# Query stores that wait for stack loads and maximum rows, batch 0's queries loaded in halves, and a subtraction behind two maxima, in a four-layer gated cross-attention network

## The reference

```python
x = x + jnp.tanh(g_xattn[0]) * _L0_xattn_ref(_layernorm(x), ctx, ctx, mask)
x = x + jnp.tanh(g_ffn[0])   * _L0_ffn_ref(_layernorm(x), ...)
x = x + jnp.tanh(g_xattn[1]) * _L1_xattn_ref(_layernorm(x), ctx, ctx, Wq, bq, Wk, bk, Wv, bv, Wo, bo)
x = x + jnp.tanh(g_ffn[1])   * _L1_ffn_ref(_layernorm(x), ...)     # 8 experts, 2 per token
...                                                                # layers 2 and 3 likewise
# the attention core of every layer:
scores = jnp.einsum('bqhd,bkhd->bhqk', q, k) * scale               # layer 0 also masks
attn = jax.nn.softmax(scores, axis=-1)
x = jnp.einsum('bhqk,bkhd->bhqd', attn, v)
```

## Time and profile before

| | |
|---|---|
| time, median of 3 runs | 1563.36 us (1557.87, 1563.36, 1565.05) |
| the profiled execution | 1561.88 us, its span 1560.0 us |
| PE busy | 1321.7 us, 85% of the span |
| PE weight load busy | 958.7 us, 61% |
| DVE busy | 963.4 us, 62% |
| ACT busy | 861.6 us, 55% |
| POOL busy | 714.5 us, 46% |
| chain that ended last | PE 68%, DVE 13%, DMA 6%, ACT 6%, issue 4% |
| mean granted TensorE clock | 0.933 of full speed |

### The profile page before, as it was taken

The page is one execution under the profiler, slowest core; times in us unless marked ns, Lnnn a source line. Parts: engine busy times, 40 slices in busy tenths (PEclk is TensorE's granted clock), DMA queues, the critical chain, the costliest instruction groups (busy, mean ns, idle before and its releaser), DMA issues.

```text
span 1560.0 us, 29423 instructions
## 1 busy us (share of the span) xinstructions
PE 1321.7 (85%) x9524; PEld 958.7 (61%) x9524; DVE 963.4 (62%) x2651; ACT 861.6 (55%) x1718; POOL 714.5 (46%) x843
## 2 busy tenths in 40 slices
PE   2599989987999489999999799848999388995985
PEld 1355479954666279999986466627887245664433
DVE  6589753335895743333337598575554277967787
ACT  2266764424887145555545488535555155885564
POOL 4366440003742677776741474258994415622000
PEclk9999999997999699999999799959999796997998
DMA  9989130048761333334147975124444498710001
GB/s 268 285 146 159 23 99 1 1 129 200 132 136 60 108 122 122 117 112 162 69 156 230 216 140 108 35 85 143 153 134 170 152 275 165 141 33 1 0 14 41
DMA packets 115568, 188.86 MB, mean 121 GB/s; under 512 B 21296, under 2 KB 91568, under 8 KB 109232
## 3 DMA queue, kind: packets, MB, share of 16 engines
q0 software_dynamic: 37056, 105.19, 28.7%
q1 hardware_dynamic: 78368, 81.79, 17.0%
HBM read 128.17 MB, written 50.20 MB: 114 GB/s over the span
## 4 chain that ended last, share of the span: by engine, by line
PE 68%; DVE 13%; DMA 6%; ACT 6%; issue 4%; POOL 1%; SPq 1%; ACTq 0%; DVEq 0%; POOLq 0%
PE PS L1212 10%; PE PS L1232 10%; PE PS L1053 9%; PE PS L1008 8%; PE PS L1012 3%; PE PS L1224 3%; DMA qk_parts<-q_parts 3%; PE PS L1090 2%; PE PS L1033 2%; PE PS L1026 2%; PE PS L1066 2%; DMA stack<-qk_parts 1%; PE PS L894 1%; PE PS L880 1%; DVE act L2593 1%
## 5 line engine op out<-in xcount | busy, mean ns | idle before, releaser
L2108 DVE TENSOR_REDUCE nm<-PS 128x2 f32<-128x512 f32 x384 | 249.9, 676 | 37.0 <-PE PS L1008 35.7
L1008 PE MATMUL PS<-stack 48*128 48x256 f32 x1024 | 214.2, 335 | 52.6 <-DVE q_parts L2043 16.2
L1008 PEld LDWEIGHTS PS<-stack 48*128 48x128 f32 x1024 | 152.9, 206 | 136.1 <-issue 57.8
L1012 PE MATMUL PS<-stack 49*128 49x256 f32 x1024 | 203.7, 321 | 0.9 <-ACT probs L1533 0.6
L1232 PE MATMUL PS<-weights,hh 128*128 x936 | 189.5, 292 | 4.5 <-DVE hl L2435 4.3
L1212 PE MATMUL PS<-weights,xh 128*128 x468 | 171.2, 421 | 11.8 <-DVE xl L2419 5.2
L680 POOL DMA_DIRECT2D stack<-mt x128 | 73.3, 573 | 216.0 <-ACT mt L1542 212.0
L1533 ACT ACTIVATE probs<-PS 128x512 f32<-128x512 f32 x256 | 145.1, 595 | 41.2 <-PE PS L1033 23.8
L1533 ACT ACTIVATE xng<-PS 128x512 f32<-128x512 f32 x256 | 145.3, 595 | 22.0 <-PE PS L1033 16.0
L1232 PEld LDWEIGHTS PS<-weights,hh 128*128 128x128 f32 x936 | 152.6, 193 | 6.5 <-issue 6.0
L1012 PEld LDWEIGHTS PS<-stack 49*128 49x128 f32 x1024 | 143.0, 195 | 10.4 <-ACT probs L1533 4.6
(11 more groups left out here) (329 smaller groups left out, 3079.3 us busy)
## 6 DMA issues: line engine op xcount, KB each, us to landing
stack<-qk_parts POOLq DMA_DIRECT2D x128, 256.0 KB, 4.1
qk_parts<-stack SPq DMA_DIRECT2D x32, 512.0 KB, 7.0
qk_parts<-q_parts SPq DMA_DIRECT2D x32, 512.0 KB, 8.3
stack<-qk_parts POOLq DMA_DIRECT2D x128, 128.0 KB, 3.8
weights<-W_dram POOLq DMA_DIRECT2D x12, 1024.0 KB
wide<-ctxT_dram SPq DMA_DIRECT2D x16, 512.0 KB, 9.4
wslot<-y_tokens SPq DMA_DIRECT2D x16, 512.0 KB, 7.5
weights<-W_dram POOLq DMA_DIRECT2D x12, 512.0 KB
```

Source lines behind the costliest of these rows:

```text
L1008: mm = pe.matmul(PS[:, u % 3, to], nat_q[:, at], nat_k, start=True, stop=True)
L1012: mm = pe.matmul(PS[:, 3 + v % 3, to], key_k[:, at], key_q, start=(l > 0 or half == 0), stop=(l > 0), skip_group_check=(l == 0))
L2108: nc.vector.tensor_reduce(nm[:, j % 2, at:at + 2], PS[:, (2 * t + h) % 3, :].rearrange("p (q n) -> p q n", q=2), AX.X, ALU.max, negate=Tru ...
```

## The change

1. **Stores held.** In layers 1 to 3 `store_q` of q1 waits for a new semaphore `stack_first` (the batch-0 keys, the ones and the first half of batch 0's queries have landed). The first part of q2 waits for maximum row 0, the second for row 1; those of q3 for rows 2 and 3. SP also waits for the store of group g - 2.
2. **Where q1's parts lie.** In layers 1 to 3 they lie in `probs` (`q_part`). So q3's high part no longer waits for q1's store (`q_place`); the first exponential does now.
3. **Halves.** In all layers batch 0's query portions are loaded by `load_queries` in two halves of four pairs of heads: 8 DMAs of 64 and 128 KB in place of 4 of 128 and 256 KB. PE's unit 0 waits for the first half, unit 8 for the second.
4. **Low part moved.** In layers 1 to 3 DVE's low part of q3 stands behind the first two maxima, and PE waits for it at the first transpose of maxima, not at unit 0.

```diff
@@ store_q (SP)
                 sp.wait_ge(qhi_done, GROUPS * l + g + 1)
                 sp.wait_ge(qlo_done, GROUPS * l + g + 1)
-                for r, part in enumerate((q_hi(g), q_lo(g))):
+                if l and g >= 2:
+                    sp.wait_ge(*stored(q_out, l, g - 2))
+                for r, part in enumerate((q_hi(l, g), q_lo(l, g))):
+                    if l and g == 1 and r == 0:
+                        sp.wait_ge(stack_first, 144 * (l + 1))
+                    if l and g >= 2:
+                        j = QUADS * l + 2 * (g - 2) + r
+                        sp.wait_ge(row_in[j % 4], 16 * (j // 4 + 1))
                     sp.dma_start(rows_of(0, r, g), by_batch(part)).then_inc(q_out[g % 2], 16)
@@ q_part, q_place (new)
+        def q_part(l, g, r):
+            if l and g == 1:
+                return probs[:].rearrange("p a n -> p (a n)").rearrange("p (r c n) -> p r c n", r=2, c=KC)[:, r].bitcast(F32R)
+            return q_parts[:, g % 2, r]
+        def q_place(l, g):
+            return stored(q_out, l, g - 4 if l and g == 3 else g - 2)
@@ load_queries (POOL, new; stands for load_stack(l, 0, 2) and load_stack(l, 0, 3))
+            def load_queries(l):
+                pool.wait_ge(*stored(q_out, l, 0))
+                for half in range(2):
+                    cs, landing = slice(PAIRS // 2 * half, PAIRS // 2 * (half + 1)), stack_in[0] if half else stack_first
+                    for h in range(2):
+                        rows = lambda r, n: stack[64 * h + DH * r:64 * h + DH * (r + n), 0, 0, cs].rearrange("p c n -> p (c n)")
+                        part = parts[0, 0, h, 0, :, cs].rearrange("p c n -> p (c n)")
+                        nc.gpsimd.dma_start(rows(2, 1), part[0:DH]).then_inc(landing, 16)
+                        nc.gpsimd.dma_start(rows(0, 2), part).then_inc(landing, 16)
@@ scores (PE)
                     if u == 0:
-                        pe.wait_ge(qlo_done, GROUPS * (l + 1))
+                        if l == 0:
+                            pe.wait_ge(qlo_done, GROUPS)
...
-                        pe.wait_ge(stack_in[b % SLOTS], 128 * loads + 16 * (l + 1))
+                        if b == 0:
+                            pe.wait_ge(stack_first, 144 * (l + 1))
...
+                    if b == 0 and c == PAIRS // 2 and h == 0:
+                        pe.wait_ge(stack_in[0], 192 * l + 64)
@@ max_rows (PE)
                 pe.wait_ge(max_done, 4 * j + 4)
+                if l and n == 0:
+                    pe.wait_ge(qlo_done, GROUPS * (l + 1))
@@ queries (ACT and DVE)
-                act.wait_ge(*stored(q_out, l, g - 2))
+                act.wait_ge(*q_place(l, g))
@@ exps (ACT)
                 act.wait_ge(sc_mm, 2 * STEPS * l + v + 1)
+                if l and v == 0:
+                    act.wait_ge(*stored(q_out, l, 1))
@@ attend (DVE)
                         maximum(l, 2 * n, 1)
+                    if l and n == 0:
+                        queries(l, GROUPS - 1)
@@ feed (DVE)
                 queries(l + 1, 2)
-                queries(l + 1, 3)
```

More of the change, by code:

```diff
@@ L177, in k_lo, with q_lo, q_hi @@
             return k_parts[:, g % 2, 1]
-        def q_lo(g):
-            return q_parts[:, g % 2, 0]
-        def q_hi(g):
-            return q_parts[:, g % 2, 1]
+        def q_part(l, g, r):
+            if l and g == 1:
+                return probs[:].rearrange("p a n -> p (a n)").rearrange("p (r c n) -> p r c n", r=2, c=KC)[:, r].bitcast(F32R)
+            return q_parts[:, g % 2, r]
+        def q_lo(l, g):
+            return q_part(l, g, 0)
+        def q_hi(l, g):
+            return q_part(l, g, 1)
         def v_heads(t, n):
@@ L635, in load_stack @@
                     nc.gpsimd.dma_start(stack[MAXROW:MAXROW + 65:64, b % SLOTS, 1].rearrange("p c n -> p (c n)"),
-                                        io["ones_rows"]).then_inc(stack_in[b % SLOTS], 16)
+                                        io["ones_rows"]).then_inc(stack_in[b] if b else stack_first, 16)
                 pool.wait_ge(*stored((q_out, k_out)[of], l, b // 2))
@@ L641, in load_stack @@
                 first, both = (0, 1) if of else (2, 0)
-                nc.gpsimd.dma_start(rows(first, 1), part[0:DH]).then_inc(stack_in[b % SLOTS], 16)
-                nc.gpsimd.dma_start(rows(both, 2), part).then_inc(stack_in[b % SLOTS], 16)
+                landing = stack_in[b % SLOTS] if b else stack_first
+                nc.gpsimd.dma_start(rows(first, 1), part[0:DH]).then_inc(landing, 16)
+                nc.gpsimd.dma_start(rows(both, 2), part).then_inc(landing, 16)
+            def load_queries(l):
[7 more added lines that the diff above has]
+                        nc.gpsimd.dma_start(rows(0, 2), part).then_inc(landing, 16)
             def scale_bo(l):
@@ L706, in _ @@
                     make_mask(0)
-                    for at in range(4):
+                    for at in range(2):
                         load_stack(0, 0, at)
+                    load_queries(0)
                     make_mask(1)
                 else:
-                    for at in range(4):
+                    for at in range(2):
                         load_stack(l, 0, at)
+                    load_queries(l)
                 for at in range(3):
@@ L985, in scores @@
                         loads = sum(x % SLOTS == b % SLOTS for x in range(B)) * l + b // SLOTS + 1
-                        pe.wait_ge(stack_in[b % SLOTS], 128 * loads + 16 * (l + 1))
+                        if b == 0:
+                            pe.wait_ge(stack_first, 144 * (l + 1))
+                        elif b % SLOTS:
+                            pe.wait_ge(stack_in[b % SLOTS], 128 * loads + 16 * (l + 1))
+                        else:
+                            pe.wait_ge(stack_in[0], 192 * (l + 1))
+                    if b == 0 and c == PAIRS // 2 and h == 0:
+                        pe.wait_ge(stack_in[0], 192 * l + 64)
                     if u >= 3:
@@ L1467, in features @@
                 if l == 0 and g >= 2:
-                    act.wait_ge(*stored(q_out, l, g - 2))
+                    act.wait_ge(*q_place(l, g))
                 for c in range(KC):
-                    ins = nc.scalar.activation(xnT[:, c, at] if l else q_hi(g)[:, c], PS[:, xT_bank(2 * l, g) + c, :], ACT.Identity)
+                    ins = nc.scalar.activation(xnT[:, c, at] if l else q_hi(l, g)[:, c], PS[:, xT_bank(2 * l, g) + c, :], ACT.Identity)
                 ins.then_inc(xT_done if l else qhi_done, 1)
@@ L2047, in queries @@
                     ins = nc.vector.scalar_tensor_tensor(
-                        q_lo(g)[:, oc], PS[:, q_bank(l, g) + oc, :], col(f"bq{l}", oc) if l != 2 else 0.0,
-                        q_hi(g)[:, oc].bitcast(F32), ALU.add, ALU.subtract)
+                        q_lo(l, g)[:, oc], PS[:, q_bank(l, g) + oc, :], col(f"bq{l}", oc) if l != 2 else 0.0,
+                        q_hi(l, g)[:, oc].bitcast(F32), ALU.add, ALU.subtract)
                 ins.then_inc(qlo_done, 1)
@@ L2086, in project @@
                             layernorm(l, 2 * l, g + 2)
-                        queries(l, g)
+                        if g + 1 < GROUPS:
+                            queries(l, g)
             def maximum(l, t, h):
```

10 lines of the change are left out of this document (5 added, 5 removed).

## The result

The changed kernel took **1546.61 us** (median of 4 runs, 1539.27 to 1551.43). The kernel before, on the same chip, took 1560.61 us (1556.79 to 1565.05). The ratio of the two is 0.9897, with a 95% interval of 0.9864 to 0.9931. Of the 7.3 us between the forecast 1553.9 and the result, 2.8 are its starting point (1563.36, the median of three runs, against 1560.61 here) and 4.5 the gain. The profiled execution took 1545.74 us against 1561.88, 16.1 us less.

The account below looks back on a forecast made before the run. The prediction took PE's matmul work as most of the time (68% of the chain), with the change touching only the seams where attention starts. Gains of 4.3, 2.8 and 2.4 us took 1563.4 to 1553.9 us; range 1547.0 to 1562.5.

Parts of the forecast that it names:

- the term for layer 0 in "Halves": Layer 0: mask and batch-1 loads move 2 us while q1's store holds the path; taken as 0, bounds -1 to +2 us.
- The three seams: Attention starts of layers 1 to 3: gains of 4.3, 2.8 and 2.4 us, together 9.5 us.
- The first half's landing: Batch 0's first half in layers 1 to 3: lands 4.2 us after issue, bounds 2.9 and the old 7.4, 6.9, 8.3.
- The store of q1: Layers 1 to 3: 10.6, 10.3 and 12.5 us until the first exponential; costs nothing, with 2 us of cover.
- What sets the ramp: Unit 0 to first key-side matmul: DVE's maxima set layer 1, a late row layer 2; ramps 9.32, 8.99, 9.32 us.
- The low part: q3's low part behind two DVE maxima in layers 1 to 3: adds 1.41 us to the ramp in each.
- Rival 1: Batch 0's first half lands no sooner, loads late by their own queue: gain 1.4 us, 1562.0 us; chance 0.13.
- Rival 2: Held q2 and q3 stores delay maximum rows and portions, 1.8 us per layer: 1559.3 us; chance 0.13.
- Rival 3: Clock stays at full level through the ramps of layers 1 to 3: gain 16.4 us, 1547.0 us; chance 0.12.
- Rival 4: q1's store lands late after 18.64 us, first exponentials stand in layers 1 to 3: +12.9 us, 1576.3 us; chance 0.07.

Follow-up runs that it names:

- e1_whole0: The changed kernel with batch 0's queries loaded whole again in layer 0 only, layers 1 to 3 as changed; ratio 0.9931 to the kernel before.
- b_again: The kernel before, unchanged, run once more for its trace alone; q1's store in layer 0 took 18.39 us, no ratio given.
- e4_nohold: The changed kernel without SP's new waits for the first half and the maximum rows; ratio 0.9934 to the kernel before.
- e6_whole123: The changed kernel with batch 0's queries loaded whole in layers 1 to 3, halves in layer 0 alone; ratio 0.9893 to the kernel before.
- e6b_whole123: Second measurement of the changed kernel with batch 0's queries whole in layers 1 to 3; ratio 0.9919 to the kernel before.
- e7_probs0: The changed kernel with q1's parts in `probs` in layer 0 too, so q3's parts wait for no store; ratio 0.9879 to the kernel before.

## Why the prediction was right, and where it was wrong

**The step that failed** is the term for layer 0 in "Halves": "I take 0, with -1 to +2 us as bounds". It saw that POOL's batch-1 loads move by 2 us while q1's store holds the path, and reasoned that the store's "total bytes stay". The bytes do stay; what changed is when the loads come, and with it how long the store takes: 11.81 us in place of 18.64. Undoing the halves there costs 5.6 us, adding them alone gives 4.5, the delay without halves 4.4, and the two traces of before and after have 6.2. With 4.5 to 5.6 us for that term the sum is 14.0 to 15.1 in place of 9.5, and the forecast 1548.3 to 1549.4. The earlier trace rows carried the warning: 18.64 us was the longest of all 320 DMAs of that tensor, whose median was 4.2. A transfer at more than four times its median, on the path, is one on which 2 us of other traffic can do much, in either direction. The bounds should have come from there: from 4.2 us of landing up to 18.64, not from the 2 us that POOL moves.

**The three seams came out near in size.** `e1_whole0`, which is the change without its layer-0 part, gained 0.69%, 10.8 us (7.0 to 14.7), where 9.5 were forecast. In the traces:

| | layer 1 | layer 2 | layer 3 |
|---|---|---|---|
| projections' end to marker, forecast | 11.8 | 10.4 | 10.7 |
| measured | 12.0 | 9.9 | 10.0 |

*The first half's landing*, taken at 4.2 us with 2.9 as its bound, was 3.0 to 3.5. The Trainium skill's fit ("DMA: Bandwidth & Descriptors", Anatomy of one DMA), 2.3 us, is too short by 0.7 to 1.2 us, as my 4.2 is too long by 0.7 to 1.2; at this place the low bound was the value to take.

*The store of q1* was said to have 2 us of cover. Its 11.17 us in layer 1 left 0.4 us before the marker, and the reckoning had forgotten ACT's table load of 1.28 us, which stood ahead of the marker before (at 377.23) and now waits for the store. The first exponential stood 0.95 us behind the marker, right behind the table load, against 0.83 before: a cost of 0.1 us, and so small by luck.

**"What sets the ramp" was misread.** It has DVE's thirteenth maximum set the marker in layer 1 and the row in layer 2 alone. By the code, unit 13 needs eleven maxima (`max_done` at u - 2) and maximum row 0. In the kernel before, the row's issue plus its landing give 379.50, 882.96 and 1297.43, and the markers stand 0.07 to 0.09 us behind. So it is at all 56 starts of attention in the fourteen traces: the marker follows the landing of row 0 by 0.04 to 0.19 us, while DVE's thirteenth maximum ends anywhere from 6.2 us ahead of it to 1.1 us behind. That it ended 0.04 us ahead of layer 1's marker was chance. The row of that layer (issue, then KB and landing), and the same in `b_again` with its marker and the four maxima of DVE around it, of which the first is the eleventh:

```profile
374.80 0.58 POOL L680 DMA_DIRECT2D stack<-mt  x1 [10.44 <-ACT mt L1542]
```

```profile
stack<-mt POOLq DMA_DIRECT2D x1, 4.0 KB, 4.7
```

```profile
375.18 0.58 POOL L680 DMA_DIRECT2D stack<-mt  x1 [12.45 <-ACT mt L1542]
...
378.81 0.58 PE L1012 MATMUL PS<-stack 49*128 49x256 f32 x1
...
378.05 2.48 DVE L2108 TENSOR_REDUCE nm<-PS 128x2 f32<-128x512 f32 x4 [0.22 <-PE PS L1008]
```

```profile
stack<-mt POOLq DMA_DIRECT2D x1, 4.0 KB, 3.5
```

The ramp is the time from unit 0 to the issue of row 0, plus its landing. Told that way the seams add up to the table of the traces, layer by layer:

| us, before and after | layer 1 | layer 2 | layer 3 |
|---|---|---|---|
| projections' end to unit 0 | 6.7, 0.2 | 3.1, -0.1 | 2.8, -0.1 |
| unit 0 to issue of row 0 | 4.57, 5.55 | 4.24, 5.19 | 5.17, 5.32 |
| landing of row 0 | 4.7, 6.2 | 5.9, 4.7 | 4.5, 4.7 |

*The low part*, taken at +1.41 us per layer, moved the issue of the row by 0.98, 0.95 and 0.15 us (and DVE's thirteenth maximum by 1.0, 0.9 and 0.8). The rows' landings, left out of the sum but for layer 2, moved by +1.5, -1.2 and +0.2. So the three markers came out near by errors that cancel: PE started 0.9 us earlier in layer 1 and the low part cost less than forecast, and row 0 of layer 1 cost 1.5 us more. In layer 1 the row took 6.1 to 7.0 us in all seven traces of kernels that have the halves and the moved low part (`e4_nohold`, without the holds, among them), 4.5 in both traces with whole loads and 4.9 with the low part ahead; which of the transfers beside it makes it late, no run isolates.

**The rivals.** *Rival 1* (the half lands no sooner) fell in the changed kernel. Its reason was half true: in `e4_nohold`, halves beside a store landed after 5.1 to 5.5 us, so the store costs a load some 2 us. That a store delays these loads but doesn't shut them out agrees with the rule of taking turns that the Trainium skill states ("DMA: Bandwidth & Descriptors", Queues, rings and completion order). *Rival 2* (rows late) had the right transfer, as the row sets every marker, but not its price: row 0 took 1.5 us longer in layer 1 and 1.0 less over the other two, and in layer 1 by another traffic: no store of q2 or q3 was under way at 362.78, but q1's, now late, and portions of batch 1. *Rival 3* (clock) did not happen as told. The granted clock was 1.00 for the first 3 to 4 us behind unit 0 (0.91 in layer 1), but 0.50 for the last 3 us ahead of the marker and the 4 us behind it in all three layers. But in layer 3 the clock rose sooner behind the marker. From 8.5 to 12.5 us behind it, the granted clock was 0.50 before; from 8.2 to 12.2 us behind it, it was 0.99 after (length, busy times, clock, DMA, GB/s):

```profile
1288.00:1292.00 4.00, 4.00 (x33) 2.28 (x32) 2.02 (x4) 2.04 (x5) 2.50 (x4) 0.50 1.17 310
1292.00:1296.00 4.00, 4.00 (x46) 2.61 (x46) 3.78 (x10) 3.58 (x10) 2.80 (x4) 0.99 1.11 267
```

That is the 3.0 us of the table. I don't count it as an effect of the change. The stretch from the marker to the transpose of the earlier trace rows was 12.7 to 14.7 us in some layers and 10.4 to 12.0 in the others, in both families: in 8 of 27 for the nine kernels that start unit 0 early, in 7 of 15 for the five that don't, and in all three layers of `e6_whole123` but in none of `e6b_whole123`, the same kernel. On the other side, layer 2's last projection matmuls took 5.25 us against 3.70, with a granted clock of 0.50 and then 0.79 where it had been 1.00, a loss of 1.5 us. *Rival 4*: its sign, ACT waiting for `qk_parts` ahead of the first exponential, stands in all three layers (3.49, 1.94 and 0.30 us), and in layer 1 the chain that ended last runs through the store, the table load and that exponential. The price was 0.1 us and not 22.4, since the store took 11.17 us and not 18.64.

## What to carry to other kernels

When a transfer that the path waits for takes several times its median, treat every other transfer near it as a term of the sum, with the whole excess as its bound; a shift of 2 us was worth 5 here, with no byte less. Hold back stores that nobody waits for until the loads on the path have landed, and then ask who is next: here the low part, then the maximum row, which gave back 1.5 us of layer 1's earlier start. Before calling an engine the one that sets a start, read in the code how many of its results the start needs, and compare the end of every candidate in more than one trace: here two ends 0.05 us apart hid the row behind DVE. Undo the parts one at a time, since the part written for one purpose may earn its time by another.

## What the runs showed of the hardware that I had not expected

- A row of 4 KB set the start of the regular loop at all 56 starts of attention. From issue to landing it took 3.5 to 7.0 us, where loads of 128 KB took 2.8 to 3.6 with no store beside them.
- q1's store of layer 0, two times 512 KB, landed after 16.2 to 18.6 us in the three traces in which the first of six software-queue loads was issued 5.2 to 5.3 us behind its start, and after 9.2 to 11.9 us in the ten in which it came 7 us or more behind (`e7_probs0`, where PE doesn't wait for it, is left out). Two us more of distance gain 4 to 9, and 5 us beyond that nothing. In the trace of before, in the 3.2 us from 34.8 on in which POOL issues these loads, the hardware queue moves only 0.10 MB; in the 4.4 us from 36.8 on in the trace of after it moves 1.12 MB beside the same loads. Two lines for each, of before and then of after (packets, MB, share of the 16 engines):

```profile
q0 software_dynamic: 99, 0.55, 82.3%
q1 hardware_dynamic: 104, 0.10, 35.9%
```

```profile
q1 hardware_dynamic: 1121, 1.12, 84.1%
q0 software_dynamic: 143, 0.35, 33.3%
```

  Why the same loads take the engines in the one case and not in the other stays open: both runs have the same mask and context loads of SP behind the store, and no experiment moved those.
- A store beside a load cost it some 2 us whether the load was 128 or 256 KB (5.3 against 3.3 us, 7.5 against 5.6, means of the three layers), and twice the bytes cost 2.3 us whether a store was there or not.
- One execution can stand 11 us from the median of its kernel (`e6_whole123`: 1562.06 profiled, 1551.16 median), and against the trace of the changed kernel 5 us of the difference lie in the attention of layer 0, whose code is the same. A difference of under 5 us between two traces needs a named wait behind it, or a second trace.
